# The last feed-forward of a two-layer network begins by halves of tokens: tiles 4 to 7 first, then tiles 0 to 3

## The reference, cut to what matters

```python
x = L0_attn_x                                   # 4 x 256 tokens, 512 wide, fp32
x = _layernorm(x + attention(x))
x = _layernorm(x + sparse_ffn(x))
x = _layernorm(x + mamba2(x))                   # the norm that the change touches
x = _layernorm(x + _L1_ffn_ref(x, Wg, Wu, Wd, ag, au, ad))

def _L1_ffn_ref(x, Wg, Wu, Wd, ag, au, ad):     # 512 -> 1376 -> 512
    gate = jnp.einsum('bsh,ih->bsi', x, Wg) * ag
    up = jnp.einsum('bsh,ih->bsi', x, Wu) * au
    h = jax.nn.silu(gate) * up
    return jnp.einsum('bsi,hi->bsh', h, Wd) * ad
```

## Time and profile before

| | us |
|---|---|
| median of 3 runs | 2508.31 |
| the three runs | 2509.47, 2508.31, 2499.82 |
| the profiled execution | 2507.97 |
| its span, first to last instruction | 2506.2 |
| busy in it: PE, DVE, ACT, POOL | 2290.8, 1690.9, 1384.0, 844.8 |
| mean granted clock of PE, share of full speed | 0.951 |

### The profile page before, as it was taken

How to read it: one execution, slowest core, us unless ns; L and a number is a source line. 1 busy time by engine, 2 the same in 40 slices (tenths; PEclk the granted TensorE clock), 3 DMA queues, 4 the chain that set the end, 5 groups by cost and what they waited for, 6 DMA issues and landing times. The chain is left out here.

```text
span 2506.2 us, 38276 instructions
## 1 busy us (share of the span) xinstructions
PE 2290.8 (91%) x11624; PEld 1637.8 (65%) x11624; DVE 1690.9 (67%) x2933; ACT 1384.0 (55%) x3121; POOL 844.8 (34%) x681
## 2 busy tenths in 40 slices
PE   6898988897999899899989999999998999987998
PEld 4554544445677676777767767676776767756877
DVE  3465555555796598489579759848966985975345
ACT  4553534314784586378368548738845864862330
POOL 4352423211353154144325414423432542441130
PEclk8699998998999899999999999999999999998999
DMA  5000000001110110111101011011101101102100
GB/s 224 10 1 9 1 1 1 1 0 61 62 31 18 52 35 27 44 30 31 42 30 35 19 48 34 28 44 30 31 15 57 30 28 47 30 1 85 42 17 34
DMA packets 38241, 85.55 MB, mean 34 GB/s; under 512 B 3584, under 2 KB 5888, under 8 KB 37376
## 3 DMA queue, kind: packets, MB, share of 16 engines
q1 hardware_dynamic: 38016, 82.82, 10.0%
HBM read 79.92 MB, written 2.88 MB: 33 GB/s over the span
## 5 line engine op out<-in xcount | busy, mean ns | idle before, releaser
L1623 PE MATMUL b_ps<-xh_keep,wh 128*128 128x512 f32 x1152 | 495.8, 430 | 22.4 <-issue 20.3
L1625 PE MATMUL b_ps<-xh_keep,wl 128*128 128x512 f32 x1152 | 468.8, 407 | 0.0
L1624 PE MATMUL b_ps<-xl_keep,wh 128*128 128x512 f32 x1152 | 468.1, 406 | 0.0
L1414 DVE TENSOR_TENSOR decayed<-decay,b_scores 128x768 f32<-128x768 f32 x256 | 397.9, 1554 | 26.0 <-ACT decay L1142 25.1
L1303 POOL TENSOR_TENSOR wl<-wraw,wh 128x512 fp32r<-128x512 f32 x144 | 190.5, 1323 | 606.6 <-ACT wh L1091 606.6
L1378 DVE SCALAR_TENSOR_TENSOR xs<-b_ps,par,xs 128x510 f32<-128x510 f32 (+2 forms) x384 | 284.9, 742 | 119.4 <-ACT xs L1110 106.4
L1136 ACT ACTIVATE decay<-b_ps,cs 128x256 f32<-128x256 f32 (+1 forms) x1024 | 345.0, 424 | 8.1 <-PE b_ps L1633 7.9
L1623 PEld LDWEIGHTS b_ps<-xh_keep,wh 128*128 128x128 f32 x1152 | 225.2, 195 | 102.1 <-issue 58.3
L1625 PEld LDWEIGHTS b_ps<-xh_keep,wl 128*128 128x128 f32 x1152 | 224.6, 195 | 54.3
L1624 PEld LDWEIGHTS b_ps<-xl_keep,wh 128*128 128x128 f32 x1152 | 226.0, 196 | 43.2
L1504 DVE SCALAR_TENSOR_TENSOR yl<-yg,par,yh 128x512 fp32r<-128x512 f32 x128 | 96.4, 758 | 202.5 <-ACT yh L1157 201.4
(11 more groups left out here) (223 smaller groups left out, 4100.9 us busy)
## 6 DMA issues: line engine op xcount, KB each, us to landing
wraw<-win_dram SPq DMA_DIRECT2D x144, 256.0 KB, 2.6
oraw<-wout_dram SPq DMA_DIRECT2D x8, 2048.0 KB, 8.9
w<-w_dram SPq DMA_DIRECT2D x2, 3584.0 KB, 23.4
fraw<-wgu_dram SPq DMA_DIRECT2D x11, 512.0 KB, 3.5
draw<-wd_dram SPq DMA_DIRECT2D x1, 2816.0 KB, 12.1
xT<-xT_dram SPq DMA_DIRECT2D x4, 512.0 KB, 3.7
x_keep<-x_dram SPq DMA_DIRECT2D x1, 2048.0 KB, 11.5
out_dram<-x_keep SPq DMA_DIRECT2D x8, 256.0 KB, 2.0
```

The lines of the kernel that those rows point to most:

```text
L1414: nc.vector.tensor_tensor(sd[:, b % 2, :, :], ex[:, b % 2, :, :], sm[:, b, :].unsqueeze(1).to_broadcast([P, 2, 3 * P]), ALU.mult)\
L1623: nc.tensor.matmul(out, w_h, x_h, start=(k == 0), stop=False)
L1624: nc.tensor.matmul(out, w_h, x_l, start=False, stop=False)
L1625: last = nc.tensor.matmul(out, w_l, x_h, start=False, stop=(k == KT - 1))
```

## The change

The order of the tokens in the prologue becomes tiles 4 to 7 (half 1) and then tiles 0 to 3 (half 0), on every engine. DVE runs `layernorm` on half 1, then waits for ACT's `xh` of each of its tiles and writes `xl`, and only then runs `layernorm` on half 0 and its `xl`. PE transposes tiles 4 to 7, then 0 to 3, both ahead of its loop. The eight waits for drained banks move from in front of the loop into the products: ahead of each half of each inner tile PE waits for the four banks of that half's tiles. Products, tanh, rounding and subtraction take half 1 ahead of half 0 in all inner tiles. The banks (`inner_jobs`), the weights' steps and the outer products stay.

```diff
--- before.py
+++ after.py
@@ -1857,12 +1857,13 @@
             return [(f"{w}{e}_{h}", 4 * e + 2 * h + n) for h in range(2) for n, w in enumerate("gu")]
 
         O_ORDER = [4, 5, 6, 7, 0, 1, 2, 3]
+        HALVES = [(1, range(NT // 2, NT)), (0, range(0, NT // 2))]
         K_ORDER = [*range(2 * KT, FT), *range(2 * KT)]
         bk = PhasedBanks(sem, "c", {"pro": [(f"xT{t}", t) for t in range(NT)], "loop": inner_jobs(0) + inner_jobs(1),
                                     "epi": inner_jobs(0) + [(f"o{t}", O_ORDER[t]) for t in range(NT)]}, loops=PAIRS)
 
         def inner(name, pro=()):
-            each = [(e, h) for e in range(2) for h in range(2)]
+            each = [(e, h) for e in range(2) for h in (1, 0)]
             return Tally(sem(name), list(pro), each, each[:2], loops=PAIRS)
 
         tanhed = inner("f_tanhed")
@@ -1922,13 +1923,13 @@
 
                 if more:
                     split(g, e + 1)
-                for h in range(2):
+                for h, _ in HALVES:
                     name = f"g{e}_{h}"
                     act.wait_ge(*bk.filled(ph, name))
                     act.sem_inc(passed)
                     nc.scalar.activation(tx[:, h, :], ps[bk.bank(ph, name)][:], ACT.Tanh, scale=sc[:, 0, ds(g * 2 + e, 1)])\
                         .then_inc(*tanhed.inc())
-                for h in range(2):
+                for h, _ in HALVES:
                     act.wait_ge(*bk.drained(ph, f"u{e}_{h}"))
                     act.sem_inc(passed)
                     nc.scalar.activation(hh[:, ds(g * 2 + e, 1), h * HALF:(h + 1) * HALF], hv[:, h:h + 1, :], ACT.Copy)\
@@ -1936,7 +1937,7 @@
 
             ph = Phase("pro", 0, 0)
             split(0, 0)
-            for t in range(NT):
+            for t in (t for _, tiles in HALVES for t in tiles):
                 act.wait_ge(*bk.filled(ph, f"xT{t}"))
                 nc.scalar.activation(xh[:, :, t * P:(t + 1) * P], ps[t][:].rearrange("p (k m) -> p k m", k=KT),
                                      ACT.Copy).then_inc(xh_done, 1)
@@ -1998,19 +1999,22 @@
                     dve.wait_ge(*bk.filled(ph, f"u{e}_{h}"))
                     nc.vector.scalar_tensor_tensor(hv[:, h, :], ps[ku][:], sc[:, 2, ds(g * 2 + e, 1)], hv[:, h, :],
                                                    ALU.mult, ALU.mult).then_inc(*bk.free(ph, f"u{e}_{h}"))
-                for h in range(2):
+                for h, _ in HALVES:
                     cols = slice(h * HALF, (h + 1) * HALF)
                     dve.wait_ge(*h_hi.made(ph, (e, h)))
                     nc.vector.tensor_tensor(hl[:, ds(g * 2 + e, 1), cols], hv[:, h:h + 1, :],
                                             hh[:, ds(g * 2 + e, 1), cols].bitcast(F32), ALU.subtract).then_inc(*h_lo.inc())
-                dve.wait_ge(*h_lo.made(ph, (e, 1)))
-
-            layernorm(nc, dve, passed, step, x, x, st, NT, lambda ins: ins.then_inc(normed, 1))
+                dve.wait_ge(*h_lo.made(ph, (e, 0)))
+
             ph = Phase("pro", 0, 0)
-            for t in range(NT):
-                dve.wait_ge(xh_done, t + 1)
-                nc.vector.tensor_tensor(xl[:, :, t * P:(t + 1) * P], ps[t][:].rearrange("p (k m) -> p k m", k=KT),
-                                        xh[:, :, t * P:(t + 1) * P].bitcast(F32), ALU.subtract).then_inc(*bk.free(ph, f"xT{t}"))
+            for i, (_, tiles) in enumerate(HALVES):
+                span = slice(tiles[0], tiles[-1] + 1)
+                layernorm(nc, dve, passed, step, x[:, span, :], x[:, span, :], st[:, span, :], len(tiles),
+                          lambda ins: ins.then_inc(normed, 1))
+                for m, t in enumerate(tiles):
+                    dve.wait_ge(xh_done, i * len(tiles) + m + 1)
+                    nc.vector.tensor_tensor(xl[:, :, t * P:(t + 1) * P], ps[t][:].rearrange("p (k m) -> p k m", k=KT),
+                                            xh[:, :, t * P:(t + 1) * P].bitcast(F32), ALU.subtract).then_inc(*bk.free(ph, f"xT{t}"))
             dve.wait_ge(loaded, 48)
             step(nc.vector.tensor_scalar(sc[:, 0, :], sc[:, 0, :], 0.5, None, ALU.mult))
             nc.vector.tensor_tensor(sc[:, 2, :], sc[:, 0, :], sc[:, 1, :], ALU.mult).then_inc(scales, 1)
@@ -2037,7 +2041,9 @@
         def _(pe):
             def tile(ph, g, e):
                 pe.wait_ge(*f_lo.made(g, e))
-                for h in range(2):
+                for h, tiles in HALVES:
+                    for t in tiles:
+                        pe.wait_ge(*bk.drained(Phase("pro", 0, 0), f"xT{t}"))
                     for w, name in enumerate("gu"):
                         name = f"{name}{e}_{h}"
                         out_ = ps[bk.bank(ph, name)][:]
@@ -2052,14 +2058,12 @@
                         last.then_inc(*bk.full(ph, name))
 
             ph = Phase("pro", 0, 0)
-            for t in range(NT):
-                pe.wait_ge(normed, t + 1)
+            for n, t in enumerate(t for _, tiles in HALVES for t in tiles):
+                pe.wait_ge(normed, n + 1)
                 pe.wait_ge(*bk.freed(ph, f"xT{t}"))
                 for k in range(KT):
                     last = nc.tensor.transpose(ps[t][:, k * P:(k + 1) * P], x[:, t, k * P:(k + 1) * P], ident)
                 last.then_inc(*bk.full(ph, f"xT{t}"))
-            for t in range(NT):
-                pe.wait_ge(*bk.drained(ph, f"xT{t}"))
             with pe.Fori(0, PAIRS) as i:
                 ph = Phase("loop", i, i)
                 tile(ph, i, 0)
```

## The result

The changed kernel took 2512.2 us in the median of 11 runs (2508.28 to 2515.99), the kernel before 2501.7 in the median of 11 (2498.73 to 2509.47). The ratio is 1.0034, with a 95% interval of 1.0021 to 1.0047: 5 to 12 us slower. The forecast was 0.22% slower, 5.6 us. That the time itself came within 1.7 us of the forecast 2513.9 is partly luck: the forecast was added to the median of three runs, 2508.3, and that of eleven is 2501.7.

What follows compares the result with a forecast made beforehand. DVE was taken to bound the prologue and PE everything behind it. First product's shift 5.05, clock 0.5, loop waits 0 and order of halves 0.05 gave 5.6 us, on 2508.3 making 2513.9 us; range 2505 to 2520.

Runs made afterwards that it cites:

- e3: The changed kernel with the outer products, their norm and stores also taking tiles 4 to 7 first; last stage 1.24 us shorter than the changed kernel's.
- e10: The changed kernel, unchanged, profiled a second time; its parts repeated within 0.2 us.
- after: The changed kernel itself, in its first profile; 2512.2 us, ratio 1.0034 to the kernel before.
- e5: The changed kernel with POOL's first subtraction waiting until DVE has scaled the first half's four tiles; first product 1.7 us earlier than in the changed kernel.
- e7: Against the kernel before: norm by halves, order 0, 1, waits inside halves, first half's products between the two groups of transpositions; ratio 0.9992, last stage 212.26 us.

## What to carry to other kernels

Splitting a prologue into halves pays only if the engine that bounds it does not repeat fixed work and does not have to wait for the round trip of the first half; look first for what can be moved without either, here the place of the waits (2.5 us) and POOL's turn (1.2 us more). For each pause of TensorE that a change lengthens or opens, ask whether the clock survives it and what the work behind it costs at half clock, also where the pause itself is absorbed. When two consumers of halves follow each other, keep one order through both.

## What was not expected of the hardware

A pause of 2.50 us after 120 us of dense products took the clock in five of six profiles, and 1.62 us in none of seven. After a pause, products one right behind the other ran at half clock for 4.7 to 5.3 us (e3, e10, after) with transpositions right ahead of them, where in e5 the clock was back 4.3 us behind the start of the transpositions.

Whether POOL or a step of DVE goes first was decided by less than 0.1 us, and changed where the stall fell and 0.2 us of its cost. In e7 POOL began 0.01 us ahead of the tenth step, and the step lasted 2.35 us instead of 0.17.
